# A vision tower on one core: routing for four token groups at once, and a new order for the first phase's VectorE and ScalarE work

## The reference

```python
# stage 1, "tok": attention inside each 4x4 patch, query = mean of the patch
x = features.reshape(b, c, h, s, w, s)
reduce_feats = x.mean((3, 5)).reshape(b, c, hw).transpose(0, 2, 1)
q = _ln(reduce_feats, ln_q_w, ln_q_b) @ Wq.T
kv = _ln(unf, ln_kv_w, ln_kv_b) @ Wkv.T
attn = softmax(einsum('bhpd,bhpnd->bhpn', q * scale, k))
h = reduce_feats + einsum('bhpn,bhpnd->bhpd', attn, v) @ proj_w.T + proj_b
# stage 2, "attn": decayed linear attention over the tokens of an image, in chunks of 128
h = _layernorm(h + lightning(h) @ w_proj + b_proj)
# stage 3, "ffn": mixture of 8 experts, the best two of each token
logits = tokens @ router_w.T
probs = softmax(logits); rw, re = top_k(probs, 2); rw = rw / rw.sum()
out = tokens + sum_e combine[:, e] * (gelu(tokens @ w1[e] + b1[e]) @ w2[e] + b2[e])
h = _layernorm(h + out)
```

## Time and profile before

| | |
|---|---|
| median of 3 runs | 2671.2 us (2666.11 to 2674.45) |
| the profiled execution's own time | 2679.64 us |
| its span | 2677.9 us |
| PE busy in the span | 2344.8 us, 88% |
| DVE busy | 1966.0 us, 73% |
| ACT busy | 1902.9 us, 71% |
| POOL busy | 1825.7 us, 68% |
| first softmax weights of phase 1 | 78.9 us |
| last of the 128 | 2201.0 us |
| mean granted TensorE clock | 0.97 of full |

### The profile page before, as it was taken

One profiled execution on the slowest core, in us unless ns is written; L12 is line 12 of the kernel. 1 busy time (PEld: TensorE's weight loads), 2 busy tenths in 40 slices (PEclk: granted clock), 3 DMA queues, 4 the chain that ended last, 5 costly groups with the idle time before them and its releaser, 6 DMA issues. The chain is left out here.

```text
span 2677.9 us, 92863 instructions
## 1 busy us (share of the span) xinstructions
PE 2344.8 (88%) x32965; PEld 1114.5 (42%) x32965; DVE 1966.0 (73%) x4552; ACT 1902.9 (71%) x4717; POOL 1825.7 (68%) x1949
## 2 busy tenths in 40 slices
PE   1788888888888888888888888888888877999997
PEld 0344444444444444444444444444444443333332
DVE  4577777777777777777777777777777766898987
ACT  3777777777777777777777777777777764555554
POOL 3678877787787787777777877877877861222323
PEclk9999999999999999999999999999999996999999
DMA  4333333333333333333333333333332200000001
GB/s 83 73 65 65 65 65 65 64 65 64 65 65 65 64 65 65 64 65 65 65 65 64 65 65 64 65 65 62 67 65 60 54 2 1 21 20 20 20 21 27
DMA packets 573723, 147.95 MB, mean 55 GB/s; under 512 B 573440, under 2 KB 573440, under 8 KB 573440
## 3 DMA queue, kind: packets, MB, share of 16 engines
q1 hardware_dynamic: 573440, 143.52, 27.4%
HBM read 135.09 MB, written 8.39 MB: 54 GB/s over the span
## 5 line engine op out<-in xcount | busy, mean ns | idle before, releaser
L709 POOL TENSOR_TENSOR pv<-vs,aw 128x512 f32<-128x512 f32 x512 | 534.9, 1076 | 431.8 <-DVE aw L923 431.8
L840 DVE TENSOR_TENSOR kqs<-ps,qqT 128x512 f32<-128x512 f32 x512 | 352.0, 688 | 317.8 <-PE ps L390 313.9
L385 PE MATMUL ps<-xb,w_ckv 64*64 64x512 f32 x2048 | 570.4, 635 | 8.3 <-DVE kqs L840 5.1
L591 ACT ACTIVATE xd<-xb 128x512 f32<-128x512 f32 x512 | 576.1, 1151 | 0.0
L390 PE MATMUL ps<-xb,w_ckv 64*64 64x512 f32 x2048 | 570.6, 635 | 0.0
L573 ACT ACTIVATE sqs<-ps 128x512 f32<-128x512 f32 x512 | 309.5, 604 | 175.0 <-PE ps L390 174.9
L862 DVE TENSOR_REDUCE agg<-pv 128x128 f32<-128x1024 f32 x128 | 251.5, 1965 | 217.3 <-POOL pv L716 217.3
L486 PE MATMUL ps<-sm,vpad 128*32 128x128 f32 x4096 | 191.8, 284 | 197.2 <-DVE kqs L840 192.5
L753 POOL TENSOR_TENSOR xt<-xb 128x512 f32<-128x512 f32 x256 | 324.6, 1268 | 21.6 <-issue 21.2
L851 DVE TENSOR_TENSOR sm<-ps,decay 128x1024 f32<-128x1024 f32 x256 | 301.6, 1220 | 28.9 <-PE ps L467 28.1
L716 POOL TENSOR_TENSOR pv<-pv 128x512 f32<-128x512 f32 x256 | 321.8, 1278 | 0.0
(11 more groups left out here) (213 smaller groups left out, 4313.4 us busy)
## 6 DMA issues: line engine op xcount, KB each, us to landing
xb<-in_x_dram SPq DMA_DIRECT2D x512, 256.0 KB, 4.3
out_dram<-outb SPq DMA_DIRECT2D x128, 64.0 KB, 1.6
w1p<-in_L_ffn_w_dram SPq DMA_DIRECT2D x16, 16.0 KB
w2p<-in_L_ffn_w_dram SPq DMA_DIRECT2D x8, 16.0 KB
b1p<-in_L_ffn_b_dram SPq DMA_DIRECT2D x8, 0.2 KB
sm<-in_L_tok_Wkv_dram SPq DMA_DIRECT2D x4, 16.0 KB, 2.0
w_av<-in_L_attn_w_qkv_dram SPq DMA_DIRECT2D x4, 16.0 KB, 2.1
b2v<-in_L_ffn_b_dram SPq DMA_DIRECT2D x4, 2.0 KB
```

What stands on the lines that cost most here:

```text
L385: nc.tensor.matmul(KB[own, :], w_ckv[own, 2 * P + m * C:2 * P + (m + 1) * C], xv[own, j], start=True, stop=True)
L591: nc.scalar.activation(xd[:, j, :].rearrange("p (b t) -> p b t", b=ST), xb[:, f, :].rearrange("p (b t d) -> p d b t", b=ST, d=ST)[:, j], A ...
L709: nc.gpsimd.tensor_tensor(pv[:, at].rearrange("p (k d) -> p k d", d=D), vs[:, s, at].rearrange("p (k d) -> p k d", d=D), aw[:, j * W4:(j + ...
L840: V.tensor_tensor(kqs[:, j, :].rearrange("p (t d) -> p t d", d=ST), KB.rearrange("p (t d) -> p t d", d=ST), qqT[:, s, :].unsqueeze(2).to_b ...
```

## The change

It has two parts.

In phase 1:
- **DVE**: the subtraction of the maximum stands ahead of `keys(3)` and no longer behind it; `aw`, its denominator and reciprocal stand right behind `keys(3)`, ahead of `hT`, `h1` and `kd` or `qdm`. `q2` is one instruction that reads the query's product from PSUM, where two read a copy. PE's `aggregated` therefore waits for `q2_done` and not for ACT's `qp_ev` before it writes over that bank.
- **ACT**: the copy `qps` and the copy into `h1` are gone. `gather(3, 0)` stands behind `ssb`, ahead of `qT` and `kT`; the chain for `yrs` (Ln, Exp, Square) stands ahead of `centred(1)` and `values(0)`, which follow it in this order; the exponential stands ahead of `centred(3)`.
- **POOL** writes its last pixel sum straight into `h1` as a sum over 16 pixels. All that is computed from it is scaled: `w_aq`, `w_ak`, `w_av` by 1/16, `bv_col` and `pb_col` by 16, `aggT` by 16/64.
- The token rows get eight more columns per image (72 = `CR` for 64): the router's logits. `w_ap`, `bp_row` and `w_av` have columns that are already multiplied by the router's matrix, so that `lt` and the scaling into `h1` carry the logits along. The router's matrix is loaded in two transfers ahead of phase 1 (28 loads for 26) and the preparation on DVE and PE has some fifteen more small operations.

In phase 2:
- PE's logits (L1116) and ACT's eviction of them (L1218) are gone; the second bias is one multiplication with 128 rows (`b2s`) for two with 64, and the gate weights are kept twice over the partitions for it.
- `choose`, `share` and the tanh serve four groups at once (`TI` = 32 rows of 8 logits on each partition for 8): once in four steps, `choose` in two parts in steps r = 0 and 1, `share` at the head of step 2, the split into float16 halves (`halved`, four operations) at the head of step 3. The routing is for the next four groups, and four steps stand ahead of the first group where there were three.

The diff, cut to its core (V is `nc.vector`). The token store:

```diff
+    CR = C + E
...
-        h1 = sb("h1", [P, UNITS, P])
+        h1 = sb("h1", [P, UNITS, 2 * CR])
```

PE in phase 1:

```diff
-                                mm = nc.tensor.matmul(B67[:, m, 0:P], red[own, :], w_qc[own, :], start=True, stop=True)
+                                mm = nc.tensor.matmul(B67[:, m, 0:P], h1[own, 4 * i + r + 1, 0:P], w_qc[own, :],
+                                                      start=True, stop=True)
...
                             pe.wait_ge(agg_done, done(i, r, 2, 1))
-                            pe.wait_ge(qp_ev, done(i, r, -1, 1))
+                            pe.wait_ge(q2_done, done(i, r, -1, 1))
```

ACT in phase 1:

```diff
                         nc.scalar.activation(ssb[:], B7, ACT.Copy).then_inc(sev_done, 1)
+                    gather(3, 0)
...
-                        nc.scalar.activation(heads(qps[:]), B67[:, :, 0:C], ACT.Copy)
                         for m in range(2):
                             ins = squares(B67[:, m, C:2 * C], ssq[:, 2 + m:3 + m], l2[:, m * C:(m + 1) * C])
                         ins.then_inc(qp_ev, 1)
-                        nc.scalar.activation(h1[:, bass.ds(4 * i + r + 1, 1), :], red[:].unsqueeze(1),
-                                             ACT.Copy, scale=1.0 / N).then_inc(rcp_done, 1)
-                    gather(3, 0)
-                    values(0)
-                    centred(1)
...
                     nc.scalar.activation(y0s[:], y0[:], ACT.Square).then_inc(rs_ch, 1)
+                    centred(1)
+                    values(0)
...
-                    centred(3)
                     if there(i, r, 1):
                         act.wait_ge(s3_done, done(i, r, 1, 1))
...
+                    centred(3)
                     gather(1, 1)
```

DVE in phase 1:

```diff
-                        for m in range(2):
-                            ins = V.tensor_scalar(q2[:, m * C:(m + 1) * C], qps[:, m * C:(m + 1) * C],
-                                                  yrs[:, 2 + m, 2:3], None, ALU.mult)
-                        ins.then_inc(q2_done, 1)
+                        V.tensor_tensor(heads(q2[:]), B67[:, :, 0:C], yrs[:, 2:4, 2:3].to_broadcast([P, 2, C]),
+                                        ALU.mult).then_inc(q2_done, 1)
...
-                    keys(3)
-                    if there(i, r, 1):
                         sbias = sgr[:, :, 25:26].rearrange("p n w -> p (n w)")
...
                                         ALU.add).then_inc(s3_done, 1)
+                    keys(3)
+                    if there(i, r, 1):
+
+                        dve.wait_ge(ex_done, done(i, r, 1, 1))
+                        dve.wait_ge(pv_ch, done(i, r, 2, ST))
+                        V.tensor_tensor(aw[:].rearrange("p (n m h) -> p n m h", m=2, h=HEADS), s4, rs_b,
+                                        ALU.mult).then_inc(aw_done, 1)
```

PE in phase 2:

```diff
-                def logits(i, r):
...
-                        nc.tensor.matmul(YB, b2h[0:64, :], cbT[0:64, r % 2, :], start=True, stop=False,
-                                         skip_group_check=True)
-                        nc.tensor.matmul(YB, b2l[0:64, :], cbT[0:64, r % 2, :], start=False, stop=False,
+                        nc.tensor.matmul(YB, b2s[:], cbT[:, r % 2, :], start=True, stop=False,
                                          skip_group_check=True)
```

DVE in phase 2:

```diff
                 def step(i, r):
-                    share(i, r)
+                    if r == 2:
+                        share(i)
+                    if r == 3:
+                        halved(i)
                     weighted(i, r, 0)
                     if gthere(i, r, 2):
                         norm(i, r)
                     weighted(i, r, 1)
-                    choose(i, r)
+                    if r < 2:
+                        choose(i, r)
                     weighted(i, r, 2)
                     weighted(i, r, 3)
```

More of the change, by code:

```diff
@@ L334, in _ @@
                     nc.tensor.transpose(ps[:, 0, j * P:(j + 1) * P], cat[:, j, :], ident[:])
+                for j in range(2):
+                    nc.tensor.transpose(ps[:, 2, j * P:(j + 1) * P], kqs[:, 0, j * P:(j + 1) * P], ident[:])
                 pe.wait_ge(s_act0, 1)
@@ L337, in _ @@
                 pe.wait_ge(s_dve0, 2)
+                for j, t in enumerate((kqs[:, 1, 0:P], w_ckv[:, 0:P], kqs[:, 1, P:2 * P])):
+                    mm = nc.tensor.matmul(ps[:, 3, j * 2 * E:(j + 1) * 2 * E], t, rt[:], start=True, stop=True)
+                mm.then_inc(s_pe0, 1)
+                pe.wait_ge(s_dve0, 3)
                 def step(i, r):
@@ L793, in _ @@
                     link(V.tensor_reduce(dst, scr[:, 3, 0:C], AX, ALU.add))
+                for t in (bv_col, pb_col):
+                    link(V.tensor_scalar(t[:], t[:], float(N), None, ALU.mult))
+                for t in (w_aq[:], w_ak[:], w_av[:, 0:2 * C]):
+                    link(V.tensor_scalar(t, t, 1.0 / N, None, ALU.mult))
                 for j, g_at in ((0, 0), (1, 2), (2, 2)):
@@ L894, in step @@
                                         ALU.add).then_inc(s3_done, 1)
+                    keys(3)
[4 more added lines that the diff above has]
+                                        ALU.mult).then_inc(aw_done, 1)
+                        V.tensor_reduce(den[:], sn.rearrange("p n j -> p j n"), AX, ALU.add).then_inc(den_done, 1)
+                        dve.wait_ge(den_done, done(i, r, 1, 1))
+                        dve.wait_ge(agg_done, done(i, r, 2, 1))
+                        link(V.reciprocal(rden[:], den[:]))
+                        assert n[0] == 5
                     if there(i, r, 2):
@@ L1020, in gdone, with batch @@
                 return i * (4 * per) + (r - lag + 1) * per + plus
+            def batch(i, ahead=0):
+                return not isinstance(i, int) or 0 <= i + ahead < G // 4
             def gthere(i, r, lag):
@@ L1025, in groups @@
             def groups(eng, step):
-                step(-1, 1)
-                step(-1, 2)
-                step(-1, 3)
+                for r in range(4):
+                    step(-1, r)
                 for r in range(4):
@@ L1188, in step @@
                     up(i, r, 2)
-                    logits(i, r)
                     spread(i, r, 1)
@@ L1265, in step @@
                     gelu(i, r, 0, 1)
-                    halves(i, r)
+                    if r == 1:
+                        halves(i)
                 groups(act, step)
@@ L1312, in choose @@
-                    link(V.tensor_reduce(at2, rb[:], AX, ALU.max))
-                    link(V.tensor_tensor(rb[:], rb[:], over_e(at2), ALU.is_equal))
-                    assert n[0] == CCH, n
-                def share(i, r):
-                    if not gthere(i, r, -1):
+                    link, n = chain(dve, rt_ch, (i + 1) * RCH + 6 * part)
+                    l = h1[:, bass.ds(16 * (i + 1), 16), :].rearrange("p k (m c) -> p (k m) c", c=CR)[:, :, C:CR]
+                    if part == 0:
+                        link(V.tensor_reduce(first, l, AX, ALU.max))
+                        link(V.tensor_tensor(ra[:], l, over_e(first), ALU.is_equal))
+                        link(V.tensor_tensor(ra[:], ra[:], rank_b, ALU.mult))
+                        link(V.tensor_reduce(at1, ra[:], AX, ALU.max))
+                        link(V.tensor_tensor(ra[:], ra[:], over_e(at1), ALU.is_equal))
+                        link(V.scalar_tensor_tensor(rest[:], ra[:], -3.0e38, l, ALU.mult, ALU.add))
+                        assert n[0] == 6
+                    else:
+                        link(V.tensor_reduce(second, rest[:], AX, ALU.max))
+                        V.tensor_tensor(gap, first, second, ALU.subtract).then_inc(gap_done, 1)
+                        link(V.tensor_tensor(rb[:], rest[:], over_e(second), ALU.is_equal))
+                        link(V.tensor_tensor(rb[:], rb[:], rank_b, ALU.mult))
+                        link(V.tensor_reduce(at2, rb[:], AX, ALU.max))
+                        link(V.tensor_tensor(rb[:], rb[:], over_e(at2), ALU.is_equal))
+                        assert n[0] == CCH - 6
@@ L1319, in share @@
+                def share(i):
+                    if not batch(i, 1):
                         return
-                    link, n = chain(dve, rt_ch, gdone(i, r, 0, RCH, CCH))
-                    dve.wait_ge(th_done, gdone(i, r, -1, 1))
-                    dve.wait_ge(tr_c, gdone(i, r, 1, 1))
+                    link, n = chain(dve, rt_ch, (i + 1) * RCH + CCH)
+                    dve.wait_ge(th_done, i + 2)
+                    if not isinstance(i, int) or i >= 0:
+                        dve.wait_ge(comb_done, i + 1)
```

191 lines of the change are left out of this document (86 added, 105 removed).

## The result

The changed kernel takes 2587.5 us (median of 4 runs, 2581.7 to 2589.5), the kernel before 2672.8 on the same chip: a ratio of 0.968, 95% interval 0.966 to 0.971. That is faster, by 85 us, and not by the 206 of the forecast's sum; the time lies 27 us above the range.

The account below looks back on a forecast made before the run. Phase 1 was taken as bound by a loop of DVE, PE and POOL waiting for each other, 16.59 us a unit. From 2679.6 us, -178 - 34 + 6 gave 2474, less 8 for the median: 2465 us, range 2410 to 2560.

Parts of the forecast that it names:

- The way from `kqs` to `aw`: Phase 1: with subtraction and exponential earlier and `h1`, `kd`/`qdm` behind it, `aw` starts 1.40 us sooner a unit, -178 us.
- the term of the moved operations: Phase 1, DVE: `h1` behind `aw`, under POOL's L709, costs 0.7 us more, but nothing on the loop.
- The softmax's order: Phase 1: subtraction ahead of the last `kqs` and exponential ahead of `centred(3)`, within the 1.40 us a unit for `aw`.
- a PE without that wait: Phase 1: without PE's 1.56 us wait for `kqs`, the period would be 15.15 us; the loop gives 15.31, taken.
- The clock: Phase 1: mean grant 0.97 loses 0.5 us a unit; a PE without the wait keeps more; taken as nothing.
- The rival "a new wait of 0.5 to 1 us a unit": Phase 1: PE gets a new wait, giving 2554 us; chance 0.18.
- its two mechanisms: Phase 1: the third gather ahead of `qT` (PE's next product waits for `kT`), or the narrow place at `q2`.
- The rival that POOL is blocked: Phase 1: both halves of `h1` hold POOL, up to 0.41 us a unit on the loop, 2517 us; chance 0.10.
- Phase 2: Phase 2: a group falls from 13.2 to 12.1 us, 32 x 1.05 = -34 us; ends -57 and -12.
- the turn to phase 2: Before phase 2's first group: a 9.6 us DVE chain replaces transposes, logits and 5.5 us of routing; zero, within 3.
- Preparation: Ahead of the first unit: two more loads, some fifteen small operations, one more turn to PE; +6 us, ends 0 and +15.

Follow-up runs that it names:

- experiment 4: On top of x1_early, the subtraction back behind `keys(3)` and the exponential back behind `centred(3)`, as before the change: 2582.5 us.
- x1_early: Against the changed kernel, `h1` and `kd`/`qdm` moved back ahead of `keys(3)` on DVE: 2473.7 us.
- x2_h1: Against the changed kernel, only the two `h1` scalings moved back ahead of `keys(3)` on DVE: 2465.9 us.
- x8_early_soft: x1_early with the subtraction back behind `keys(3)` and the exponential back behind `centred(3)`, as before the change: 2582.5 us.

## Why the prediction was wrong, point by point

- **The way from `kqs` to `aw`**: right. `aw` stands 0.72 us behind the last `kqs`, ACT was not late by more than 0.4 us in all (one wait in the whole span), and PE's wait at L490 is 0.24 us.
- **The step that failed** is the term of the moved operations: "It lies between `aw` and the masks, and DVE waited 0.85 us for PE at the next `keys(0)`: nothing on the loop." It failed in size and in place. In size: I had +0.7 us for `h1` and nothing for `kd`/`qdm`, which stood in the same move; measured are +0.9 to +1.6 for the one and +0.93 for the other. In place: the slack that I took is the one at `keys(0)`, behind the masks, but a wait of PE hangs on the first mask, ahead of that. In the kernel before, DVE's masks waited for PE 6.9 us in 38 units, 0.18 us a unit, and the first was through 0.3 us ahead of PE: that was the slack. Counted from the last `kqs`, the masks came 1.3 us later in the change (5.15 us behind it for 3.83 on average). So PE's wait was not taken away but moved: 1.56 us at L486 before, 1.46 at L456 after, with the same 1.81 us idle a unit. Undoing `h1`'s move alone gives 2465.9 us and a period of 15.21, where the prediction had 2465 and 15.31.
- **That agreement is partly luck.** The softmax's order gave 0.86 us of the period (experiment 4), not 1.40, and the other 0.59 come from terms that I had at nothing, the clock among them. The luck is that they sum to about 1.4. The 15.15 that I had for a PE without that wait was close.
- **The clock** came back from 0.97 to 1.00, and I took nothing for it. By the rule of the Trainium skill (TensorE: Matmul & The Clock Gate, Part 1) a PE that is less idle keeps the clock. From the kernel before to the change the trace doesn't bear this out: the clock rose with 1.81 us idle a unit in both. In x1_early and x2_h1 PE is idle for 0.87 and 0.82 us and has 1.00, which fits; but x8_early_soft has 1.00 with 1.50 us idle. So idle time alone does not tell the clock here.
- **The rival "a new wait of 0.5 to 1 us a unit"** is what happened, by neither of its two mechanisms: the wait is 1.46 us, and the gather ahead of `qT` gained time and didn't cost any. `q2` made no wait.
- **The rival that POOL is blocked**: L709 grew from 1076 to 1086 ns, 0.04 us a unit for the 0.41 that I priced. The Trainium skill (SBUF — State Buffer, its section on the two separate sides and the one on who interferes with whom) says that whoever starts first holds the shared pair for its whole instruction and that the other fully blocks. Among the forms that can contend it names `tensor_scalar`, which is `h1`, and an operation with two SBUF inputs, which is `kd` and `qdm`. The trace agrees on DVE's side, to 0.15 us; on POOL's side the longest of its products took 1137 ns for 1067 of the shortest. I took it for a surcharge on `h1`, and it is a wait for the end of an instruction of another engine.
- **Phase 2**: 25 us for 34. A group takes 12.3 us for 12.1 (between the first products of five in a row 12.8, 12.4, 11.9 and 12.1). Right in kind, mis-sized by 0.2 us a group, 6 us in all. The other 3 us are the turn to phase 2: from the last `aw` to the first product of a hidden value and a gate it takes 53.3 us for 50.7, and I had it at zero. (From 13.2 to 12.1 are 1.1 us a group, or 35 us; the forecast's sum has 1.05 and 34.)
- **Preparation**: +0.8 us for +6, inside its bounds.

## What to carry to other kernels

Where an instruction of VectorE moves under GpSimd's work, count every instruction that moves with it, and price each by up to the duration of one GpSimd instruction, not by a factor; the operations here that read one of two inputs from PSUM stood there unharmed. Then ask which engine waits for the next thing that VectorE signals, not for the next place where VectorE itself waits. And when two delays lie ahead of the same wait, undoing either may give most of the gain, so a test of one alone says what it is worth, but not what the other costs.
